# An embedding and compressed-interaction network with top layers: more warm-up matmuls, and the first x_rep loads in another order

## The reference

```python
e = jnp.stack([tbl_f[ids[:, f]] for f in range(39)], axis=1)        # (1024, 39, 16)
x0 = xk = e
for idx, (W, b) in enumerate([(w0, b0), (w1, b1), (w2, b2)]):
    z = jnp.einsum('bhd,bkd,hks->bsd', x0, xk, W) + b[None, :, None]   # 128 units
    z = relu(z)
    if idx != 2:
        xk = z[:, :64, :]
        direct.append(z[:, 64:, :])
    else:
        direct.append(z)
logit = jnp.sum(jnp.concatenate(direct, axis=1), axis=-1)              # (1024, 256)
h = concatenate([logit, dense_ctx], axis=1)                           # 272 columns
y = relu(relu(h @ W_top1 + b_top1) @ W_top2 + b_top2) @ W_top3
```

## Time and profile before

| what | value |
|---|---|
| median of 3 executions | 1269.59 us (1266.67 to 1270.83) |
| the profiled execution, its own time | 1268.23 us |
| span of its records | 1266.4 us |
| mean granted TensorE clock | 0.984 of full speed |
| PE busy / DVE busy / POOL busy / ACT busy | 97% / 92% / 71% / 56% |

### The profile page before, as it was taken

How to read it: one execution, slowest core, us unless ns; L and a number is a source line. 1 busy time by engine, 2 the same in 40 slices (tenths; PEclk the granted TensorE clock), 3 DMA queues, 4 the chain that set the end, 5 groups by cost and what they waited for, 6 DMA issues and landing times.

```text
span 1266.4 us, 15522 instructions
## 1 busy us (share of the span) xinstructions
PE 1231.7 (97%) x4256; PEld 783.5 (62%) x4256; DVE 1165.7 (92%) x1045; ACT 707.7 (56%) x741; POOL 900.8 (71%) x569
## 2 busy tenths in 40 slices
PE   4879999999999999999999999999999999999999
PEld 2446666666666666666666666666666666666664
DVE  7479999989999999999999999999999999999991
ACT  1245655556565655556655655557555565565552
POOL 7676777876878787787877778787878755654540
PEclk7789999999999999999999999999999999999999
DMA  7699878777998888888988888889888888897510
GB/s 210 151 167 222 202 180 187 180 196 191 219 213 178 185 190 197 201 200 210 215 178 185 192 193 201 203 210 219 177 181 195 194 200 198 206 219 174 134 51 0
DMA packets 135922, 234.42 MB, mean 185 GB/s; under 512 B 16403, under 2 KB 25101, under 8 KB 135787
## 3 DMA queue, kind: packets, MB, share of 16 engines
q1 hardware_dynamic: 84335, 151.67, 52.1%
q10 hardware_dynamic: 41994, 79.99, 24.8%
q0 software_dynamic: 9568, 2.47, 2.1%
HBM read 230.21 MB, written 6.23 MB: 187 GB/s over the span
## 4 chain that ended last, share of the span: by engine, by line
PE 83%; DMA 5%; DVE 4%; POOL 3%; SPq 2%; issue 2%; ACT 1%; DVEq 0%; ACTq 0%; POOLq 0%
PE z_odd L1041 33%; PE z_even L1041 31%; PE z_even L1075 7%; PE z_odd L1075 6%; DMA x_rep<-x_rows 2%; DVE whole L889 2%; DMA x_shift<-x_rows 2%; POOL rest L583 2%; PE whole_psum L1069 1%; DVE whole_psum L889 1%; PE x_odd L1095 1%; POOL gathered L568 1%; PE x_even L1095 1%; SPq L441 1%; DVE rest L906 1%
## 5 line engine op out<-in xcount | busy, mean ns | idle before, releaser
L583 POOL TENSOR_TENSOR rest<-whole,head 128x1024 fp32r<-128x1024 f32 x256 | 611.2, 2398 | 247.8 <-ACT head L701 247.2
L889 DVE TENSOR_TENSOR whole<-x_banks,x_rep 128x1024 f32<-128x1024 f32 x448 | 534.1, 1216 | 35.7 <-ACT x_banks L659 30.7
L701 ACT CAST head<-whole 128x1024 fp32r<-128x1024 f32 x256 | 268.6, 1049 | 159.0 <-DVE whole L889 120.7
L568 POOL DMA_INDIRECT gathered<-in_tbl,idx x299 | 286.7, 959 | 82.2 <-issue 74.1
L701 ACT CAST head<-whole_psum 128x1024 fp32r<-128x1024 f32 x192 | 194.8, 1015 | 142.0 <-DVE whole_psum L889 135.8
L889 DVE TENSOR_TENSOR whole_psum<-x_banks,x_rep 128x1024 f32<-128x1024 f32 x192 | 235.5, 1226 | 5.8 <-DMA x_rep<-x_rows 3.5
L906 DVE TENSOR_TENSOR rest<-whole_psum,head 128x1024 fp32r<-128x1024 f32 x192 | 234.5, 1222 | 0.3 <-ACT head L701 0.3
L1041 PE MATMUL z_odd<-head,w_rest 128*128 128x512 f32 x427 | 198.0, 464 | 3.9 <-POOL rest L583 3.3
L1041 PE MATMUL z_even<-head,w_rest 128*128 128x512 f32 x405 | 186.3, 460 | 1.0 <-DVE rest L906 0.8
L1041 PE MATMUL z_odd<-whole,w_whole 128*128 128x512 f32 x400 | 185.3, 592 | 0.5 <-DVE whole L889 0.5
L1041 PE MATMUL z_odd<-head,w_head 128*128 128x512 f32 x460 | 182.5, 397 | 0.0
(11 more groups left out here) (117 smaller groups left out, 1001.5 us busy)
## 6 DMA issues: line engine op xcount, KB each, us to landing
x_rep<-x_rows ACTq DMA_DIRECT2D x128, 512.0 KB, 11.7
x_rep<-x_rows SPq DMA_DIRECT2D x128, 512.0 KB, 11.7
x_shift<-x_rows SPq DMA_DIRECT2D x93, 546.0 KB
x_rep<-x_rows ACTq DMA_DIRECT2D x32, 384.0 KB
x_rep<-x_rows SPq DMA_DIRECT2D x32, 384.0 KB
x_rep<-x_rows SPq DMA_DIRECT2D x32, 256.0 KB
gathered<-in_tbl,idx POOLq DMA_INDIRECT x299, 7.0
x_rows<-xt_and_ctx SPq DMA_DIRECT2D x32, 78.0 KB
```

What stands on the lines that cost most here:

```text
L568: nc.gpsimd.indirect_dma_start(gathered[:, f, :], None, tables[f], bass.IndirectOffsetOnAxis(ap=idx[:, f:f + 1], axis=0)).then_inc(s_gathe ...
L583: nc.gpsimd.tensor_tensor(rest[:, split_slot(product)], whole_slot(product), head[:, split_slot(product)].bitcast(F32), ALU.subtract).then ...
L701: nc.scalar.copy(head[:, split_slot(product)], src).then_inc(s_head, 1)
L889: nc.vector.tensor_tensor(out[0:rows, 0:width, :], xk[0:rows, :].unsqueeze(1).to_broadcast([rows, width, N]), x0, ALU.mult).then_inc(s_pro ...
```

## The change

Three edits, all effective only at the start of the program. `WARM_UP` goes from 10 to 26, which adds 16 matmuls. ACT's issues for groups 0 and 1 of tile 1 move from behind the heads of products 1 and 2 to behind those of products 7 and 9, in the first tile alone. SP's half of group 0 of tile 0 is issued ahead of the indices and of the rows of tile 1.

```diff
-WARM_UP = 10
+WARM_UP = 26
@@ SP, body(t)
                 if has_layer0(t) and not first:
 
                     load_rep(t, range(TWICE))
+                if first:
+                    load_rep(t, [0])
                 load_indices(t)
...
                     if first:
-                        load_rep(t, range(LOADS))
+                        load_rep(t, range(1, LOADS))
                         sp.wait_ge(s_prod, before(t, 0, PAIRS0))
@@ ACT, body(t)
-                    heads(t, 1, start=n, upto=n + 1, loads={1: [0], 2: [1]} if has_layer0(t) else {})
+                    early = {7: [0], 9: [1]} if is_first(t) else {1: [0], 2: [1]}
+                    heads(t, 1, start=n, upto=n + 1, loads=early if has_layer0(t) else {})
```

## The result

The changed kernel takes 1272.92 us (median of 19 runs, 1269.78 to 1274.96), the kernel before 1268.80 us (19 runs, 1265.49 to 1271.49). The ratio is 1.0029, with a 95% interval from 1.0020 to 1.0038: slower by 0.29%, some 3.7 us (4.1 us by the two medians). That is about the 0.3% that the prediction calls the least that can be told from no change, but the whole interval lies above 1. The forecast was 1265.1 us, a gain. On two further chips the change or its warm-up edit alone loses about as much; on another one the change gains 0.14%. Most of this document is about what divides them.

What follows compares the result with a forecast made beforehand. The prediction took PE, 97% busy, as the bound, with only idle and low-clock time in the first 100 us to win. 6.2 won less 1.7 given back makes 4.5 us: 1263.7 profiled, 1265.1 us median, 8-in-10 range 1261.5 to 1269.5.

Steps and rivals of the forecast that it cites:

- They fit into the idle time.: Before tile 0's selects: 26 warm-ups take about 5.7 us, ending at 41.7, before PE is needed at 41.98.
- The rival on the other side: Slower: warm-ups at the low clock take 11.1 us and delay transposes 5.1 us; 1273.6 us, chance 0.06.
- The clock's rise: After PE's restarts the full clock was expected back 4.1 to 6.8 us later; its rise may differ between runs.
- The clock in the selects: Tile 0's selects: warm-ups hold the clock up, four records take about 1.9 us, x1 comes some 5 us earlier.
- which changes little, since POOL covers it: Tile 0: selects at the low clock would matter little, as layer 1 waits for POOL's gathers ending at 68.4.
- The restart behind the longer wait: Layer 1 of tile 0: PE waits about 8 us, restarts at 70.87 with the clock down; taken as minus 0.8 us.
- SP's order: Group 0 of tile 0 moves up 1.6 us or so; costed at zero, hidden by the wait for POOL.
- ACT's late issues: Layer 0 of tile 1: x_shift lands at 85.0 instead of 87.7, layer 0 ends at 92.3, 6.2 us won.
- the other case: If ACT's halves run from the moment of issue beside SP's queue, x_shift for tile 1 lands at 86.2 to 86.6.
- What is given back: Layer 1 of tile 1: PE waits for POOL's rest of product 5; 1.7 us of the gain is lost.
- The cushion: PE's slack ahead of POOL's rests in layer 1 of tile 1, expected to shrink by 3.6 us and break.
- the step that decides: Moving ACT's halves later lets SP's queue land x_shift at 85.0, so layer 0 of tile 1 wins 6.2 us.

Runs made afterwards that it cites:

- e1_warm26: Only WARM_UP 10 to 26, against the kernel before: 1272.84 us, ratio 1.0025.
- e10_warm26_again: Only WARM_UP 10 to 26, repeated on another chip, against the kernel before: 1272.99 us, ratio 1.0029.
- e9_change_again: The whole change, all three edits, repeated on another chip against the kernel before: 1272.33 us, ratio 1.0025.
- e11_before_third: The kernel before, unchanged, profiled a third time, against the kernel before on the same chip: 1268.23 us, ratio 0.9997.
- e6_warm42: Only WARM_UP 10 to 42, against the kernel before: 1268.52 us, ratio 1.0022.
- e3_sp_first: Only SP's half of group 0 of tile 0 issued ahead of the indices and rows, against the kernel before: 1268.94 us, ratio 0.9994.
- e17_change_third: The whole change, all three edits, a third time on another chip, against the kernel before: 1264.92 us, ratio 0.9986.
- e15_warm2_act_sp: ACT's and SP's edits with WARM_UP 2 instead of 10, against the kernel before: 1264.45 us, ratio 0.9984.
- e18_warm2_again: ACT's and SP's edits with WARM_UP 2, repeated on another chip, against the kernel before: 1265.11 us, ratio 0.9991.
- e16_act_late_first40: ACT's edit alone with FIRST_WARM_UP 24 to 40 and 10 warm-ups, against the kernel before: 1265.64 us, ratio 1.0006.
- e2_act_late: Only ACT's halves of groups 0 and 1 of tile 1 behind the heads of products 7 and 9, against the kernel before: 1270.39 us, ratio 1.0005.
- e4_act_sp: ACT's and SP's edits together, WARM_UP left at 10, against the kernel before: 1269.73 us, ratio 1.0005.
- e12_act_sp_again: ACT's and SP's edits with WARM_UP 10, repeated on another chip, against the kernel before: 1269.51 us, ratio 1.0011.
- sets 1 and 3: Eight runs, four on each of two chips: edits alone or combined, the whole change, the unchanged kernel; against the kernel before, 1269.38 and 1268.65 us.
- sets 2, 4 and 5: Ten runs on three chips: other warm-up counts, edit combinations, rewritten small loads, the change, the unchanged kernel; against the kernel before, 1266.54, 1265.66 and 1265.94 us.
- e8_first40_all: All three edits plus FIRST_WARM_UP 24 to 40, against the kernel before: 1263.48 us, ratio 0.9982.

## Why the prediction was wrong

**The step that failed: "They fit into the idle time."** The prediction put the 16 more warm-ups, 3.4 us of PE, into the 3.67 us that PE idles for ACT's copy. That gap isn't a property of the kernel. It is there when the one-hot sums end at 35.3, and gone when the stall makes them end at 44.4, since the copy and the warm-ups then start together at 44.8. The copy takes 1.75 us, ten warm-ups 2.33, 26 of them 5.8: ten overrun the copy by 0.4 us, 26 by 3.8. Shown by e1_warm26 and e10_warm26_again (the edit alone costs 3.5 and 4.3 us over their sets' kernel before), by e9_change_again beside e11_before_third, and from the other side by e6_warm42, which overruns without the stall and loses 2.0 us by its medians. The sum had 0 for this term at the transposes and minus 0.8 for the clock; on a chip with the stall it is minus 3.1 to minus 4.0 at the transposes (e9_change_again and e10_warm26_again less e11_before_third), and x_shift for tile 1 lands later with it.

The one profile at hand couldn't show the stall. Still, the slack in it was 41.98 less 41.7, 0.3 us for 3.4 us of added work, and the prediction gave a late end a chance of 0.06 only.

**The rival on the other side** named the right place (transposes later, so the first head, POOL's first rest and x_shift later; 1273.6 us against 1272.92) and the wrong mechanism. The warm-ups didn't run at the low clock: 26 took 5.78 to 6.30 us in every profile that has them, where the rival had 11.1. Its number is near the measured one by luck: it has the transposes at 47.1, and they stand at 50.89, of which 5.1 us are there with ten warm-ups too (e11_before_third less).

**The clock's rise.** Where the stall precedes them, the warm-ups start behind sums at 0.50 (in the window 40 to 42 us of the change), and the rise falls a little differently from run to run: ten take 2.33 us in e11_before_third and 2.98 in e3_sp_first, 26 take 5.79 in e1_warm26 and 6.23 in e10_warm26_again. The Trainium skill, TensorE: Matmul & The Clock Gate, Part 1, which was cited for such differences, says that the point at which the clock rises differs from run to run; these runs agree, with 0.4 to 0.7 us at stake in the warm-ups, not the 5 that the rival gave it. What differed by more there is the stall, of which the prediction had nothing.

**The clock in the selects** was half right. The first groups of e17_change_third run at the full clock (1.97 us at 43.74), the later ones don't (3.76 at 50.55). In the change with the stall the first are fast too (1.97 us at 52.49), and so is e11_before_third with ten warm-ups, which had no idle time ahead of the transposes. In e17_change_third they hardly matter: POOL's first rest begins at 68.49, against 68.44, and x_shift is issued at 59.97, against 60.41 by the same view. But "which changes little, since POOL covers it" doesn't hold in every run, and the prediction had no term for it. In e15_warm2_act_sp the granted clock is 0.50 in each 4 us from 44 to 68. Layer 0 of tile 0 is late there, x_shift is issued at 65.14, and POOL's first rest starts at 74.65, behind ACT's head. e18_warm2_again is the same kernel on another chip; its clock is back by 56 us, and the two rows stand at 60.70 and 68.34. Over all profiles the issue of x_shift begins anywhere between 59.29 and 66.93. Such a delay need not reach the end: the ratios of these two are 0.9984 and 0.9991.

**The restart behind the longer wait** was sized about right. PE does wait longer for POOL's first rest in e11_before_third, 7.90 us, and from its restart at 75.19 to the end of layer 1 at 90.82 it takes 15.6 us, where before it was 14.5 (70.87 to 85.34). That is 1.2 us dearer, for the 0.4 to 1.7 of the sum. In e17_change_third the wait is 3.56 us and nothing is dearer.

**SP's order** was costed at zero, and e3_sp_first gives 0.9994 [0.9979, 1.0009], with the stall. Without it the edit wasn't run alone. The runs without the stall that have it beside ACT's lie at 0.9982 to 0.9991, and e16_act_late_first40, which lacks it, at 1.0006. So a part of the small gain may be SP's; the intervals overlap, and it isn't shown.

**ACT's late issues.** Where there is no stall, the landing of x_shift came out as worked out: about 83.8 for 85.0, layer 0 over at 91.4 for 92.3, with ACT's issues near 76 and 80. (The landing of 86.2 to 86.6 in the other case comes out as 86.0 to 86.7 from its own terms; nothing hangs on it.) With the stall and 26 warm-ups it brought nothing to be seen: x_shift takes 27.93 us with all three edits, 27.32 with the warm-ups alone (e1_warm26). The rate of 0.165 to 0.205 MB/us that the prediction took for SP's queue alone fails there. In 78 to 88 us of the change SP's queue is nearly alone and moves 0.13 MB/us. DMA queues of that stretch, q1 SP's and q10 ACT's:

```profile
q1 hardware_dynamic: 672, 1.31, 98.8%
q10 hardware_dynamic: 47, 0.09, 6.1%
```

Ten us of 16 engines at 98.8% for 672 packets are 235 ns for each. In 62 to 72 us (shown at the end) it is 16 x 10 x 0.489 / 779, 100 ns. Why a packet of the same 2 KB takes longer here is open.

**What is given back** was mis-sized and named at another link. The prediction had 1.7 us, from a POOL rest in layer 1 of tile 1. e17_change_third gives back 6.3, of which 5.8 are read at the same layer, from an x_rep group that lands late, and the low clock behind the wait is half of it. The cushion that the prediction reckoned with was POOL's alone; the transfers run through at a DMA share over 1.0 from 100 to 120 us. As I read it, PE's being earlier by 7 us doesn't make their bytes earlier; no run tested that by itself. Something alike shows with the stall. Beside e3_sp_first on their chip (layer 0 over at 97.12, the second at 128.84), e2_act_late and e4_act_sp are over at 97.08 and 95.94 and start the second at 133.20 and 131.33. Beside e11_before_third (97.99 and 129.41), e12_act_sp_again has 96.56 and 131.96. With ACT's edit layer 0 ends at the same time or earlier, and the second starts 2.5 to 4.4 us later.

**In sum**: without the stall the step that decides was right and the gain at the end is some 1 us, not 4.5 (1264.92 against 1265.94). With it, the term put at nothing costs 3.5 us (e1_warm26) and decides the sign.

**Left open.** What the stall is. It is in the result's profile and in every profile of sets 1 and 3, and in none of sets 2, 4 and 5 nor in the one that the prediction read, so it goes with the chip or its hour, not with the edits. The one-record steps in it lie close to multiples of 0.7 us (31.17, 32.58, 33.32, 34.73, 36.82, 38.21, 38.91, 40.31). The queue that loads instructions moves one packet of 16 KB in this stretch. In e17_change_third it comes at 33.3 us, in the result's profile at 41.4, some 1 us behind the end of the stall, each time when some 50 of the sums have run. So it isn't what ends the stall. Whether the kernel before loses by the stall can't be told from its sets' medians (1268.65 to 1269.38 with it, 1265.66 to 1266.54 without), since the chips may differ in more. Two warm-ups on a chip with the stall weren't tried, nor 40 first warm-ups.

No version here was shown to beat both kernels on both kinds of chip. The lowest ratios without the stall are those of e8_first40_all, 0.9982 and 0.9984, and e15_warm2_act_sp's 0.9984 can't be told from them; with the stall the kernel before is as good as any that was run.

## What to carry to other kernels

Matmuls without use go in front of the critical engine's next work, so they are free only while something else is later. Read how long the cover is in several executions, and on several chips if that can be had: here a cover of 3.67 us was there on some and 0 on others, and an edit that just fits one profile has no margin for the other. And when a stage is made earlier on the engine that bounds, follow the bytes of the stage behind it: if the queues were full already, the time can come back as a new wait, with the low clock behind it.

## What the runs showed of the hardware

PE can all but stop in a row of short matmuls with nothing that the profile shows to wait for: 12 or 13 of 116 ran, then three to nine records in some 8 us, then the rest in 4 us. Two chips did this in each of four profiles, three others in none of four, four and two.

In one stretch two queues together moved far more than one. DMA queues of the change, 62 to 72 us, with SP's x_shift and x_rep and ACT's halves:

```profile
DMA packets 1894, 3.11 MB, mean 311 GB/s; under 512 B 258, under 2 KB 417, under 8 KB 1893
## 3 DMA queue, kind: packets, MB, share of 16 engines
q10 hardware_dynamic: 800, 1.54, 52.2%
q1 hardware_dynamic: 779, 1.48, 48.9%
```

That is 311 GB/s for the two (and a little from POOL's gathers), against 142 GB/s in 78 to 88 us, where SP's queue was nearly alone, and 205 GB/s in the earlier trace rows. It isn't so everywhere: in the earlier trace rows the two moved 1.30 MB in 6 us, 217 GB/s. SP's own 1.48 MB in 10 us are what it moves alone in the slow stretch or better. So ACT's halves beside SP's cost SP less than the earlier trace rows had made me think, at least there. The Trainium skill, DMA: Bandwidth & Descriptors, Issuing engines are not separate DMA queues, says that issuing from several engines saves only the issue time. In this case the bytes per us were twice as many with two queues at work in 62 to 72 us as with one in 78 to 88, and hardly more in the earlier trace rows than in the earlier trace rows; whether the second queue is the reason, or the kind of the transfers, no run here tells.
